# Query vectors of a local attention left unnormed: their norm moves into the softmax

## The reference, cut to what matters

```python
q, k, v = (to_heads(q), to_heads(k), to_heads(v))
q = l2norm(q) * qs
k = l2norm(k) * ksc
q, k = rotary_xpos(q, k)
...
sim = jnp.einsum('bhwid,bhwjd->bhwij', bq, bk)        # bq = 8 * q
sim = jnp.where(mask, -jnp.finfo(sim.dtype).max, sim)
attn = jax.nn.softmax(sim, axis=-1)
out = jnp.einsum('bhwij,bhwjd->bhwid', attn, bv)
```

## Time and profile before

| | us |
|---|---|
| median of three executions | 618.06 |
| the profiled execution, its own time | 617.46 |
| its span in the profile | 615.5 |
| busy: TensorE matmuls | 502.9 (82%) |
| busy: VectorE | 456.7 (74%) |
| busy: ScalarE | 347.5 (56%) |
| busy: GpSimd | 308.3 (50%) |
| first exponential of the first layer starts | at 130.68 |
| last exponential of the second layer starts | at 433.1 |

### The profile page before, as it was taken

The page is one execution under the profiler, slowest core; times in us unless marked ns, Lnnn a source line. Parts: engine busy times, 40 slices in busy tenths (PEclk is TensorE's granted clock), DMA queues, the critical chain, the costliest instruction groups (busy, mean ns, idle before and its releaser), DMA issues. The chain is left out here.

```text
span 615.5 us, 11720 instructions
## 1 busy us (share of the span) xinstructions
PE 502.9 (82%) x4010; PEld 315.0 (51%) x4010; DVE 456.7 (74%) x1201; ACT 347.5 (56%) x998; POOL 308.3 (50%) x248
## 2 busy tenths in 40 slices
PE   6640014689999998799789999999799877999996
PEld 5320002247776766444247777766444333666774
DVE  5899998788999984545789999983445676367776
ACT  4860002469999995633568999995733423633331
POOL 6550001588888886647488888882100255030000
PEclk9885556799999999799989999999899989899999
DMA  8300001011111112000111111111000000000001
GB/s 295 116 2 0 1 1 65 4 27 43 38 36 36 36 37 78 1 2 1 48 30 36 37 44 37 36 36 27 2 2 0 0 1 1 0 1 2 18 23 30
DMA packets 14193, 18.89 MB, mean 31 GB/s; under 512 B 2186, under 2 KB 8628, under 8 KB 14004
## 3 DMA queue, kind: packets, MB, share of 16 engines
q1 hardware_dynamic: 13844, 18.04, 10.7%
q10 hardware_dynamic: 288, 0.08, 0.1%
HBM read 8.94 MB, written 1.05 MB: 16 GB/s over the span
## 5 line engine op out<-in xcount | busy, mean ns | idle before, releaser
L480 ACT ACTIVATE prob<-psS,nmx 128x128 f32<-128x128 f32 x256 | 90.1, 377 | 23.1 <-DVE nmx L1026 23.1
L605 POOL TENSOR_TENSOR rst<-mv,half 128x4 f32<-128x4 f32 x24 | 24.8, 1035 | 148.3 <-DVE mv L824 134.1
L744 POOL TENSOR_TENSOR rn<-ssq,half 128x16 f32<-128x16 f32 x32 | 93.2, 2913 | 3.9 <-DVE ssq L1012 0.9
L736 POOL TENSOR_TENSOR ra<-ra,rb 128x512 f32<-128x512 f32 x64 | 80.2, 1274 | 2.9 <-DVE rb L994 2.9
L1310 PE MATMUL psQK<-wqkv,hsA 128*128 128x512 f32 x128 | 64.1, 625 | 3.8 <-ACT z L360 2.7
L354 ACT ACTIVATE lnx<-psT,nmr,rst 128x128 f32<-128x128 f32 x52 | 19.6, 459 | 83.6 <-POOL nmr L606 83.5
L480 ACT ACTIVATION_READ_ACCUMULATOR prob<-psS,nmx 128x1 f32 x256 | 55.0, 215 | 0.0
L1026 DVE TENSOR_REDUCE nmx<-psS 128x4 f32<-128x512 f32 x64 | 41.0, 683 | 15.4 <-PE psS L1394 15.4
L752 POOL TENSOR_TENSOR qkn<-ra,rn 128x512 f32<-128x512 f32 x32 | 33.4, 1043 | 34.3 <-DVE qkn L1020 34.3
L991 DVE TENSOR_TENSOR ra<-psQK,rope 128x512 f32<-128x512 f32 x64 | 43.9, 686 | 4.4 <-PE psQK L1310 3.8
L994 DVE TENSOR_TENSOR rb<-psQK,rope 128x512 f32<-128x512 f32 x64 | 43.6, 681 | 0.0
(11 more groups left out here) (228 smaller groups left out, 1214.8 us busy)
## 6 DMA issues: line engine op xcount, KB each, us to landing
vAB<-vAB SPq DMA_DIRECT2D x62, 128.0 KB, 2.2
wqkv<-in_wqkv SPq DMA_DIRECT2D x2, 768.0 KB, 7.8
big<-in_x SPq DMA_DIRECT2D x4, 256.0 KB, 4.7
ropeb<-in_rope SPq DMA_DIRECT2D x1, 1024.0 KB, 6.0
big<-in_ew SPq DMA_DIRECT2D x2, 512.0 KB, 4.3
out<-big SPq DMA_DIRECT2D x4, 256.0 KB, 2.3
wmod<-in_wmod SPq DMA_DIRECT2D x2, 384.0 KB, 6.2
w<-in_w SPq DMA_DIRECT2D x2, 341.0 KB
```

The source lines that it names most:

```text
L480: act.activation(prob[:, k, :], psS[:, hb, c * P:(c + 1) * P], ACT.Exp, bias=nmx[:, k:k + 1], accum_out=sums[:, n % 2, k:k + 1]).then_inc( ...
L736: pool.tensor_tensor(o, o, rb[:, r], ALU.add).then_inc(s["sum_" + name], 1)
L744: pool.tensor_tensor(rn[:, :], ssq[:, :], half[:, :], ALU.pow).then_inc(s["rn_ready"], 1)
```

## The change

The norm of q is no longer applied to q. The raw rotated q is transposed (`ra_q` in place of `qkn`), so the scores come out unnormed. `rn` (the norms) gets two buffers. The negated maxima are multiplied by the norm (one more VectorE instruction for each half, on 128x4 values, after a wait of VectorE for its own reduction), and the exponential takes the norm as its `scale` operand, a value for each partition, beside the bias. `q_normed` and its semaphore go away, and with them the waits of GpSimd for it. New waits: `negmax` for `rn_ready`, `norms` for the exponentials of tile n-2 (they read the buffer of `rn` that it will write), `turn_qk` for `sum_q`, and `rope_products` of q for `qT_fill`.

```diff
-        rn = sb("rn", [P, 16])
+        rn = sb("rn", [P, 2, 16])
...
                     act.activation(prob[:, k, :], psS[:, hb, c * P:(c + 1) * P], ACT.Exp, bias=nmx[:, k:k + 1],
-                                   accum_out=sums[:, n % 2, k:k + 1]).then_inc(s["p_ready"], 1)
+                                   scale=rn[:, n % 2, 2 * c + hb:2 * c + hb + 1], accum_out=sums[:, n % 2, k:k + 1]).then_inc(s["p_ready"], 1)
...
                 if n:
                     pool.wait_ge(s["k_ready"], n)
-                    pool.wait_ge(s["q_ready"], n)
-                pool.tensor_tensor(rn[:, :], ssq[:, :], half[:, :], ALU.pow).then_inc(s["rn_ready"], 1)
+                if n >= 2:
+                    pool.wait_ge(s["p_ready"], 8 * (n - 1))
+                pool.tensor_tensor(rn[:, n % 2, :], ssq[:, :], half[:, :], ALU.pow).then_inc(s["rn_ready"], 1)
...
                 if has(i + 2):
                     norms(n + 2)
-                    pool.wait_ge(s["q_ready"], n + 3)
                     k_normed(n + 2)
...
                 if n >= 2:
-                    dve.wait_ge(s[name + "_ready"], n - 1)
+                    dve.wait_ge(s[("qT_fill", "k_ready")[part]], n - 1)
...
-            def q_normed(n):
-
+            def negmax(n, hb):
+
+                dve.wait_ge(s["s_done"], 2 * n + hb + 1)
+                half_max = nmx[:, 4 * hb:4 * hb + 4]
+                own.one(dve.tensor_reduce(half_max, psS[:, hb, :].rearrange("p (h k) -> p h k", h=4),
+                                          AX.X, ALU.max, negate=True))
                 dve.wait_ge(s["rn_ready"], n + 1)
-                dve.wait_ge(s["sum_q"], n + 1)
-                if n:
-                    dve.wait_ge(s["qT_fill"], n)
-                dve.tensor_tensor(heads(qkn[:, 0:INNER]), heads(ra_q[n % 2]), rn[:, 0:8].unsqueeze(2).to_broadcast([P, H, DH]),
-                                  ALU.mult).then_inc(s["q_ready"], 1)
-
-            def negmax(n, hb):
-
-                dve.wait_ge(s["s_done"], 2 * n + hb + 1)
-                dve.tensor_reduce(nmx[:, 4 * hb:4 * hb + 4], psS[:, hb, :].rearrange("p (h k) -> p h k", h=4),
-                                  AX.X, ALU.max, negate=True).then_inc(s["negmax"], 1)
+                dve.tensor_tensor(half_max, half_max, rn[:, n % 2, hb:8:2], ALU.mult).then_inc(s["negmax"], 1)
...
-                if has(i + 2):
-                    q_normed(n + 2)
...
-                pe.wait_ge(s["q_ready"], n + 1)
+                pe.wait_ge(s["sum_q"], n + 1)
...
-                four(psT0, lambda k: qkn[:, k * P:(k + 1) * P]).then_inc(s["qT_fill"], 1)
+                four(psT0, lambda k: ra_q[n % 2][:, k * P:(k + 1) * P]).then_inc(s["qT_fill"], 1)
```

More of the change, by code:

```diff
@@ L185, in program @@
             dve dve_b act_own pool_own fallback fallback_b rope_ready tabs_phase tabs_ready z_ready hsA_ready
-            k_mm q_mm sq_k sq_q ssq_k ssq_q rope_k rope_q sum_k sum_q ssq_max rn_ready q_ready k_ready
+            k_mm q_mm sq_k sq_q ssq_k ssq_q rope_k rope_q sum_k sum_q ssq_max rn_ready k_ready
             v_fill v_evac qT_fill qT_evac kT_fill kT_evac pT_fill pT_evac oT_fill oT_evac
@@ L751, in k_normed @@
                     pool.wait_ge(s["kT_fill"], n)
-                pool.tensor_tensor(heads(qkn[:, INNER:]), heads(ra_k[n % 2]), rn[:, 8:16].unsqueeze(2).to_broadcast([P, H, DH]),
+                pool.tensor_tensor(heads(qkn[:, INNER:]), heads(ra_k[n % 2]), rn[:, n % 2, 8:16].unsqueeze(2).to_broadcast([P, H, DH]),
                                    ALU.mult).then_inc(s["k_ready"], 1)
@@ L1012, in clamped @@
                 dve.tensor_scalar(ssq[:, :], ssq[:, :], 1e-24, None, ALU.max).then_inc(s["ssq_max"], 1)
-            def q_normed(n):
-                dve.wait_ge(s["rn_ready"], n + 1)
-                dve.wait_ge(s["sum_q"], n + 1)
-                if n:
-                    dve.wait_ge(s["qT_fill"], n)
-                dve.tensor_tensor(heads(qkn[:, 0:INNER]), heads(ra_q[n % 2]), rn[:, 0:8].unsqueeze(2).to_broadcast([P, H, DH]),
-                                  ALU.mult).then_inc(s["q_ready"], 1)
             def negmax(n, hb):
                 dve.wait_ge(s["s_done"], 2 * n + hb + 1)
-                dve.tensor_reduce(nmx[:, 4 * hb:4 * hb + 4], psS[:, hb, :].rearrange("p (h k) -> p h k", h=4),
-                                  AX.X, ALU.max, negate=True).then_inc(s["negmax"], 1)
+                half_max = nmx[:, 4 * hb:4 * hb + 4]
+                own.one(dve.tensor_reduce(half_max, psS[:, hb, :].rearrange("p (h k) -> p h k", h=4),
+                                          AX.X, ALU.max, negate=True))
+                dve.wait_ge(s["rn_ready"], n + 1)
+                dve.tensor_tensor(half_max, half_max, rn[:, n % 2, hb:8:2], ALU.mult).then_inc(s["negmax"], 1)
             def o_scaled(n):
```

## The result

The changed kernel takes 634.9 us (median of four executions, 632.5 to 637.4) against 617.8 of the kernel before (four, 616.6 to 622.7): ratio 1.027 [1.020, 1.034], slower. The forecast was 626.8 with a range of 620 to 635, so the sign was right and the size (+9.0 us) half of what came (+17.1). The profiled execution took 632.96 us with a span of 631.0, which is 15.5 more than the span of before.

What follows compares the result with a forecast made beforehand. It took a GpSimd-VectorE ring of waits, 7.34 us a tile, as the bound. 26 x 0.41 = 10.7, less 2 x 2.3, plus 2 x 1.3 gave +8.7, so 626.2, median 626.8 us; range 620 to 635.

Steps and rivals of the forecast that it cites:

- The q product and GpSimd's wait: Steady tile: removing the product saves 0.61 us on VectorE and the 0.80 GpSimd idled for it, opening the old ring.
- The scale operand: Eight exponentials on ScalarE: 0.094 us more each, so 0.75 more a tile, to 3.52.
- the old ring: GpSimd and VectorE before the change: norm power, q product, k product, rope additions, clamp, next power; 7.34 us a tile.
- The chain without the port: Steady tile, ScalarE to TensorE to VectorE to ScalarE: 0.90, 1.21, 1.11, 0.72, 0.22 and 3.52, sum 7.68 us.
- The port: SBUF access held by VectorE or GpSimd while the other waits: delays the first small product to 7.53, period 7.68 to 7.75.
- the ring through the power: Power waits until 3.7 us after the first exponential; k product at 6.63 frees the port at 7.53; exponentials at 7.75.
- The starts of the layers: First exponentials of each layer come sooner: -2.3 us for each layer, bounds -1.5 and -4.
- The ends: End of each layer: +0.6 step to tile 14, +0.5 next step, +0.2 last tile; together +1.3 us, bounds 0.5 and 2.
- The attention as a whole: All terms, both layers: 26 x 0.41 = 10.7, less 2 x 2.3, plus 2 x 1.3, so +8.7 us.
- No port conflict: Rival: small products never wait for GpSimd; 7.68 us a tile, +6.6 us, 624.7 us; chance 0.18.
- Fetch hidden: Rival: operand fetch hides beside the exponentials' read-out; TensorE sets 7.1 to 7.34 us a tile, 614 us; chance 0.15.
- Gap missed: Rival: first small product asks after the k addition starts at 7.63 and sits it out; +1.64 a tile, 658.7 us; chance 0.07.

Runs made afterwards that it cites:

- experiment 8: Changed kernel with an immediate scale of 0.01 on the exponentials and the small product's second input from PSUM (values wrong): ratio 0.993 to the kernel before, tile 7.25 us.
- experiment 5: Kernel before the change, with a scale operand of ones added to its eight exponentials, all else kept: ratio 1.009 to the kernel before, tile 7.41 us.
- experiment 2: Changed kernel, but the small product multiplies by zero and reads its second input from PSUM, without subtraction of the maximum: ratio 1.011 to the kernel before, tile 7.57 us.
- experiment 3: Changed kernel with three buffers of norms and the small product's second input from PSUM (multiplying by zero): ratio 1.012 to the kernel before, tile 7.57 us.
- 6: Kernel before the change, without GpSimd's wait for the q product ahead of the k product: ratio 0.996 to the kernel before, tile 7.21 us.
- experiment 7: Kernel before the change, with only tiles 0 and 1 of each layer done the change's way: 620.3 us against 618.6, ratio 1.003.
- experiment 1: Changed kernel with three buffers of norms, so the power no longer waits for the exponentials just running: 629.7 us, ratio 1.021 to the kernel before, tile 7.66 us.
- experiment 9: Kernel before without GpSimd's wait for the q product, and with both maxima ahead of the q product on VectorE: 645 us, ratio 1.042, tile 8.18 us.

## Why the prediction was right in sign and small in size

- **The q product and GpSimd's wait** went as said, and bought little together: 0.09 of a tile with both new costs gone (experiment 8).
- **The scale operand**, 0.094 taken from two gelu rows: exponentials start 0.437 apart where it was 0.346, so 0.091, eight of them 3.50 in place of the 3.52 taken. Right. So is its worth by itself: nearly hidden (7.34 to 7.41 in experiment 5), because the old ring did not pass through ScalarE. The Trainium skill, "ScalarE: Activation LUTs", section "What ACT_TABLE_LOAD costs", says that each pointer operand for the partitions adds about 93 ns; the rows agree, also with a sum read out behind each exponential.
- **The chain without the port**, 7.68: it measured 7.57 (experiments 2 and 3). Of the 0.11, 0.06 lie between q copy and scores (2.05 for 2.11): I had taken 0.90 between q copy and turning from a kernel in which TensorE came late, and it is 0.79 in the timeline of after, with 1.26 behind it for 1.21. The rest is 0.01 or 0.02 in each other term. A distance read at a full engine is not a latency.
- **The port** was the right mechanism with its place right: the first product waits for the k product's release at 0.90, the second for the addition's at 1.13. The mis-sized term is the way to it: the power starts 3.80 after the first exponential, not 3.7, and the k product follows 2.98 later, not 2.93 (3.80 + 2.98 + 0.90 + 0.20 against 3.7 + 2.93 + 0.90 + 0.22). That is the whole step from 7.75 to 7.88, 0.13 a tile and 3.4 us. I had treated the ring through the power as a phase within a chain of 7.68, with a collision of 0.07, when it is itself the longest ring: every tenth on it counts in full, and the chain that I summed with care has 0.31 of slack. The bound of 7.9 held it. By the rule of the Trainium skill's "SBUF — State Buffer", section "SBUF: two separate sides", a lock held for the whole instruction, the prediction had worked out 7.89. That is nearly the measured number, but with the measured terms the same rule gives 3.80 + 2.98 + 1.04 + 0.20 = 8.02; the rows have the small product through 0.14 sooner (below), and the closeness is chance.
- **The starts of the layers**: -2.3 each forecast, -3.3 and -2.6 measured, inside the bounds, but by other parts. In layer one the first scores come 6.99 after the first power (118.91 to 125.90), 9.08 before (117.53 to 126.61): 2.1 sooner, where I had put "some tenths". From there to the exponentials it is 2.85 for the 2.05 expected (4.07 before), since the maxima still stand behind rope products on VectorE:

```profile
125.90 1.04 PE L1386 MATMUL psS<-kT,qT 64*64 64x128 f32 x32
127.24 0.67 DVE L994 TENSOR_TENSOR rb<-psQK,rope 128x512 f32<-128x512 f32 x1
127.84 0.68 DVE L1018 TENSOR_REDUCE nmx<-psS 128x4 f32<-128x512 f32 x1
```

- **The ends**: +1.1 for each layer without its last tile, +1.24 measured (+0.83 and +0.41). TensorE's wait for the scaled o grew from 0.86 to 1.26, 0.40 for the 0.5 expected; experiment 8, with neither port wait nor operand, has that step as long (10.88, 10.49 before), and experiment 5, with the operand alone, has it as before (10.48): so it goes with what the changed kernels share, the two more instructions in front among them, as I had it. The other half was reasoned wrongly: I held the step to tile 14 to be TensorE's, not stretched by exponentials, and the operand alone stretches it from 8.42 to 9.05 (experiment 5). But 6 and 8, with cheap exponentials, have 8.88 and 8.97, so what sets that step stays open. For the last tile I had +0.2; its exponentials are 0.7 longer, and from their end to layer two it is no less (50.34 us after, 50.09 before).
- **The attention as a whole**: +10.6 measured, +8.3 forecast (8.7 less 0.2 for each last tile, which lies outside those points). **The other 4.9 us** are, but for the 0.2 of each last tile, in no term. 3.4 of them lie in code that is the same in all kernels, and such differences come and go with TensorE's granted clock. The stretch from the last tile of layer two to the end, same columns as above, of before, of experiment 7, of after and of experiment 3:

```profile
430.70:615.50 184.80, 163.23 (x753) 97.39 (x749) 110.26 (x338) 70.22 (x140) 31.77 (x34) 0.97 0.02 7
```

```profile
429.10:614.00 184.90, 163.25 (x753) 97.45 (x749) 110.22 (x338) 70.14 (x140) 31.80 (x34) 0.97 0.02 7
```

```profile
443.66:631.00 187.34, 165.37 (x747) 97.98 (x743) 110.43 (x339) 70.98 (x140) 31.80 (x34) 0.94 0.02 6
```

```profile
433.70:623.70 190.00, 168.26 (x747) 100.72 (x743) 110.36 (x339) 70.88 (x140) 31.71 (x34) 0.93 0.02 6
```

The same VectorE work (110.3 us) takes 184.8 us at a granted clock of 0.97 and 190.0 at 0.93. The clock is at its lower level, 1.2 GHz, three times in that stretch of before and five times in that of after, besides the very end. In after one of these times is from 518.0 to 521.4 us, and two 128x512 matmuls take 1.91 there:

```profile
519.00:521.00 2.00, 2.00 (x4) 0.82 (x3) 0.75 (x1) 2.00 (x7) 1.00 (x2) 0.50 0.00 0
```

In the 6 us up to 518.0 TensorE was busy 3.96 us, at 2.4 GHz. In before it was busy 3.98 of 6 us ahead of the same piece of code, and there it kept 2.4 GHz, with 1.02 for such a pair. The clock also differs between executions of one kernel: of the four of after, 632.5 us went with a mean granted clock of 0.923 and 637.4 with 0.911. That the change moves the drops to its disadvantage is not shown: one profile each says where they fell, not why. By the medians (+17.1 us) the part outside the attention is about 6.5; the interval of the ratio stands for +12.5 to +21 us, and the attention with the last exponentials, 12.1, lies just below it.

**What was luck.** The terms of the sum held within the bounds, the steady tile at 7.88 near the edge of 7.9. The median of 634.9 stays inside 635 although some 5 us of it belong to no term; with the sum's own upper bound, 634, it would have been outside. The largest step that failed by size is the ring through the power, 0.13 a tile; what the total missed beyond that is mostly outside the code that the prediction was about.

**The rivals.** No port conflict: fell, the products are 0.47 and 0.59 long. Fetch hidden: fell, 0.437 apart. Gap missed: did not come; the first product asks at 183.41, 0.41 before the k addition starts.

## What to carry to other kernels

When a new wait closes a ring through a slow instruction (here exponentials, power, k product), sum that ring first and in full, since it, not the chain of operands, may be the longest. A VectorE instruction with two SBUF inputs costs what stands on the port beside it, however few elements it has: ask who comes first, and give a tiny one on the path an input in PSUM, as experiment 2 did. An earlier start of a stage can be lost again in the next steps (experiment 7); look whether the ring that sets its pace begins there.

## What the runs showed of the hardware

- In these rows the port goes to whoever asks first, in both directions: a GpSimd product drawn from 1.04 to 1.55 by a VectorE product that began 0.04 before it; a VectorE product of 0.69 drawn to 1.52 by a GpSimd addition that began 0.28 before it.
- A blocked VectorE instruction ends 0.14 sooner than the recorded end of the GpSimd one plus its own time: 1.13 of 1.27 and in experiment 1, 0.90 of 1.04 in after, 1.12 of some 1.26 in experiment 9. The texts here put that as a port free 0.14 early; the rows can't tell it from 0.14 of the blocked instruction that passes while it waits.
- A product of 128x4 takes 0.16, and 0.47 or 0.59 when it meets such an instruction; as SCALAR_TENSOR_TENSOR with its second input in PSUM 0.16 in the midst of a GpSimd product.
- The clamp waits too, with one input and its output in SBUF: 0.17 alone (experiment 1), 0.30 in the earlier trace rows, and 1.17 in after, where it starts 0.12 behind an addition on GpSimd:

```profile
130.94 1.17 DVE L1012 TENSOR_SCALAR ssq<-ssq 128x16 f32<-128x16 f32 x1
```

- The reductions of the squares (L1005), also with one SBUF input, do not wait: in experiment 1 they take 0.67 to 0.69 each, the 37 with a GpSimd instruction beside them and the 27 without.
